# One Mamba scan with a routed feed-forward layer: two more of the 32 state terms of a block on ScalarE, the two parts of y added by TensorE, and a shifted table of slots

## The reference

```python
xz = xn @ in_proj_w.T                    # x_s and z, 512 channels each
u  = silu(conv4(x_s) + conv_b)
dt, B, C = split(u @ x_proj_w.T)         # 16, 16, 16
delta = softplus(dt @ dt_proj_w.T + dt_proj_b)
h = exp(delta * A) * h + delta * u * B   # per channel and each of 16 states, over time
y = sum over the states of h * C  + u * D_param
attn = (y * silu(z)) @ out_proj_w.T + residual
ffn  = top-2 of 8 experts, each (silu(x @ w1) * (x @ w3)) @ w2
x = x + attn + ffn
```

## Time and profile before

| what | value |
|---|---|
| median of 3 runs | 2661.89 us (2659.11 to 2669.71) |
| the profiled execution, its own time | 2653.93 us |
| its span | 2652.2 us |
| VectorE busy | 2459.2 us, 93% |
| TensorE busy (matmul) | 2292.8 us, 86% |
| GpSimd busy | 2031.0 us, 77% |
| ScalarE busy | 1658.9 us, 63% |
| mean granted TensorE clock | 0.936 |

### The profile page before, as it was taken

One profiled execution on the slowest core, in us unless ns is written; L12 is line 12 of the kernel. 1 busy time (PEld: TensorE's weight loads), 2 busy tenths in 40 slices (PEclk: granted clock), 3 DMA queues, 4 the chain that ended last, 5 costly groups with the idle time before them and its releaser, 6 DMA issues. The chain is left out here.

```text
span 2652.2 us, 47132 instructions
## 1 busy us (share of the span) xinstructions
PE 2292.8 (86%) x14442; PEld 1986.7 (75%) x14442; DVE 2459.2 (93%) x4041; ACT 1658.9 (63%) x4137; POOL 2031.0 (77%) x1607
## 2 busy tenths in 40 slices
PE   3958789899999999998999989999989899998665
PEld 2855578878787887877888877888877787887554
DVE  7679999999999999999999999999999999999997
ACT  3940566666666666666666666666666666666653
POOL 3430678888888888888888888888888888888883
PEclk7858899999999999999999999999999999999776
DMA  7216045565555555555555555555555555542451
GB/s 244 92 40 216 29 124 156 154 176 152 161 151 152 157 160 171 158 157 153 155 160 155 166 163 151 158 156 160 154 162 164 156 152 157 159 113 52 96 100 32
DMA packets 267099, 379.38 MB, mean 143 GB/s; under 512 B 21492, under 2 KB 158324, under 8 KB 266852
## 3 DMA queue, kind: packets, MB, share of 16 engines
q1 hardware_dynamic: 236196, 332.26, 40.2%
q0 software_dynamic: 28480, 43.94, 10.1%
q10 hardware_dynamic: 2176, 0.18, 0.1%
HBM read 332.59 MB, written 52.10 MB: 145 GB/s over the span
## 5 line engine op out<-in xcount | busy, mean ns | idle before, releaser
L475 POOL TENSOR_TENSOR h<-du,bbc 128x512 f32<-128x512 f32 x1024 | 1362.5, 1354 | 505.3 <-PE HT L1305 375.3
L1071 DVE TENSOR_TENSOR_SCAN h<-DA,carry,h 128x256 f32<-128x256 f32 x2048 | 1417.7, 734 | 91.4 <-ACT DA L748 79.0
L748 ACT ACTIVATE DA<-delta,alog 128x256 f32<-128x256 f32 x2048 | 882.6, 468 | 212.2 <-DVE h L1071 200.9
L1305 PE MATMUL HT<-ident,h 128*128 128x128 f32 x4096 | 665.8, 288 | 260.5 <-DVE yT L1082 259.1
L1305 PEld LDWEIGHTS HT<-ident,h 128*128 128x128 f32 x4096 | 496.6, 148 | 416.2 <-issue 375.2
L1082 DVE SCALAR_TENSOR_TENSOR yT<-HT,cT,yT 128x512 f32<-128x512 f32 x960 | 698.5, 728 | 3.1 <-PE HT L1305 3.1
L1354 PE MATMUL G<-xtT,W 128*128 128x128 f32 x2160 | 273.2, 281 | 0.0
L1368 PE MATMUL G<-W,fill 128*128 128x256 f32 x1080 | 271.8, 397 | 0.0
L1361 PE MATMUL G<-xtT,W 128*128 128x128 f32 x2160 | 263.4, 275 | 0.0
L1354 PEld LDWEIGHTS G<-xtT,W 128*128 128x128 f32 x2160 | 261.1, 198 | 0.0
L1361 PEld LDWEIGHTS G<-xtT,W 128*128 128x128 f32 x2160 | 252.2, 192 | 0.0
(11 more groups left out here) (183 smaller groups left out, 2986.6 us busy)
## 6 DMA issues: line engine op xcount, KB each, us to landing
W<-in_w_T_dram SPq DMA_DIRECT2D x405, 512.0 KB, 4.2
bbc<-b_dram SPq DMA_DIRECT2D x256, 256.0 KB, 4.3
xraw<-in_x_dram SPq DMA_DIRECT2D x64, 256.0 KB, 2.7
xn_dram<-W SPq DMA_DIRECT2D x8, 1032.0 KB, 14.0
W<-in_x_dram SPq DMA_DIRECT2D x32, 256.0 KB, 6.7
moe_dram<-fill SPq DMA_DIRECT2D x32, 256.0 KB, 4.0
out_dram<-tmpA SPq DMA_DIRECT2D x32, 256.0 KB, 2.2
out_dram<-moe_dram POOLq DMA_DIRECT2D x32, 256.0 KB, 4.4
```

Source lines behind the costliest of these rows:

```text
L475: pool.tensor_tensor(h[:, v % RING], du[:, b, 2 * q:2 * q + 2, :], bbc[:, s // 2 % BRING, s % 2, :].unsqueeze(1).to_broadcast([P, 2, T]), ...
L748: i = act.activation(DA[:, v % 2, k, :], delta[:, b, c, :], ACT.Exp, scale=nega[:, c, s:s + 1])
L1071: i = dve.tensor_tensor_scan(h[:, v % RING, k, :], DA[:, v % 2, k, :], h[:, v % RING, k, :], carry[:, b, s, c:c + 1], ALU.mult, ALU.add)
L1305: i = pe.transpose(HT[:, k, c * P:(c + 1) * P], h[:, (2 * s + c // 2) % RING, c % 2, k * P:(k + 1) * P], ident[:, :])
```

## The change

The terms u = 24 and 25 (state 12) are also made by ScalarE, in every block but the first. `first_state` becomes `state(j, b, u)`. The new terms go into their own buffer yS, which lies in a scratch area, with table entries second0 = 27 and second1 = 28. VectorE's adds of these two terms are gone; it has none in steps 28 and 29 any more. In `y_mm` each matmul of yT against the identity is preceded by one of yS, into the same sum: four more in each of the two calls. `by_act` and `added` say which terms are ScalarE's and which semaphore count stands for a term.

The table moves too: normalise 6 to 3, xs1 10 to 9, exp 22 to 21, ln 23 to 22, sp0 and sp1 24, 25 to 23, 24, wm 23 to 22, corr 24 to 23, delta 26 to 25, du 27 to 26, cT 25 to 24 and its copy 26 to 25, out1 29 to 28, result 31 to 30. `SCATTER` is 9 instead of 8. `MULT`, `Y` and `YO` are now given for each tile of a block: the first tile's are one step later (5, 6, 7), and so are the fourth tile's Y and YO (6, 7).

```diff
+        yS = scratch[4].rearrange("p (k d) -> p k d", k=NT)
...
-                 "first0": 3, "first1": 4, "y0": 4, "gate_y0": 6, "y1": 5, "gate_y1": 7, "out0": 27, "out1": 29,
-                 "oacc": 17, "result": 31,
-                 "normalise": 6, "transpose": 7, "copy_xT": 8, "xs0": 8, "copy_xs0": 9, "xs1": 10, "copy_xs1": 12,
+                 "first0": 3, "first1": 4, "second0": 27, "second1": 28, "y0": 4, "gate_y0": 6, "y1": 5, "gate_y1": 7, "out0": 27, "out1": 28,
+                 "oacc": 17, "result": 30,
+                 "normalise": 3, "transpose": 7, "copy_xT": 8, "xs0": 8, "copy_xs0": 9, "xs1": 9, "copy_xs1": 12,
                  "conv0": 11, "conv1": 12, "conv2": 13, "conv3": 14, "tanh_u0": 13, "silu_u0": 14, "tanh_u1": 15, "silu_u1": 16,
-                 "x_proj": 17, "copy_xdbc": 18, "dt": 19, "abs": 20, "exp": 22, "ln": 23, "sp0": 24, "sp1": 25,
-                 "wm": 23, "corr": 24, "delta": 26, "du": 27, "cT": 25, "copy_cT": 26}
+                 "x_proj": 17, "copy_xdbc": 18, "dt": 19, "abs": 20, "exp": 21, "ln": 22, "sp0": 23, "sp1": 24,
+                 "wm": 22, "corr": 23, "delta": 25, "du": 26, "cT": 24, "copy_cT": 25}
...
+        def by_act(n):
+            return (0, 1, 24, 25) if n else (0, 1)
+        def added(n, u):
+            if u < 0:
+                n, u = n - 1, u + U
+            if n < 0:
+                return s_acc, 0
+            mine = sum(i <= u for i in by_act(n))
+            earlier = 4 * n - 2 if n else 0
+            if u in by_act(n):
+                return s_y0, earlier + mine
+            return s_acc, U * n - earlier + u + 1 - mine
...
-        XT, XT_COPY, H1, H3, TANH, A2, MULT, Y, YO, SCATTER = 0, 1, 2, 3, 3, 4, 4, 5, 6, 8
+        XT, XT_COPY, H1, H3, TANH, A2, SCATTER = 0, 1, 2, 3, 3, 4, 9
+        MULT, Y, YO = (5, 4, 4, 4, 4), (6, 5, 5, 6, 5), (7, 6, 6, 7, 6)
...
-                act.activation(yT[:, b, k, :], HT[:, k, :], ACT.Identity, scale=cT[:, b, k, 0:1]).then_inc(s_y0, 1)
+                wait(act, s_ymm, 2 * (n - 1) if s == 0 else 2 * n)
+                if n == 1 and s:
+                    act.wait_ge(s_idx, 1)
+                act.activation(yS[:, k, :] if s else yT[:, b, k, :], HT[:, k, :], ACT.Identity,
+                               scale=cT[:, b, k, s:s + 1]).then_inc(s_y0, 1)
...
-                if u in (2, 3):
-                    pe.wait_ge(s_y0, 2 * n + u - 1)
-                else:
-                    wait(pe, s_acc, 30 * n + u - (1 if u < 2 else 3))
+                wait(pe, *added(n, u - 2))
...
+                        if n:
+                            pe.matmul(dst[:, m, k * P:(k + 1) * P], yS[:, k, c * P:(c + 1) * P], ident[:, :],
+                                      start=False, stop=False, skip_group_check=True)
                         i = pe.matmul(dst[:, m, k * P:(k + 1) * P], yT[:, b, k, c * P:(c + 1) * P], ident[:, :],
                                       start=False, stop=True, skip_group_check=True)
```

More of the change, by code:

```diff
@@ L240, in tile_of @@
             for k in range(PER):
-                at = U * (k // len(XT_UNITS)) + XT_UNITS[k % len(XT_UNITS)] + stage
+                at = U * (k // len(XT_UNITS)) + XT_UNITS[k % len(XT_UNITS)]
+                at += stage[k % len(XT_UNITS)] if isinstance(stage, tuple) else stage
                 for pair in (0, 1, -1):
@@ L698, in copy_cT, with state @@
                 act.wait_ge(s_btmm, n + 1)
-                wait(act, s_acc, 30 * (n - 1))
+                wait(act, *added(n - 2, U - 1))
                 act.copy(cT[:, b], FB[:, :, R + NS:ROWS]).then_inc(s_ct, 1)
-            def first_state(j, b, k):
+            def state(j, b, u):
                 n = number(j, b)
-                act.wait_ge(s_htr, 32 * n + k + 1)
+                s, k = divmod(u, 2)
+                act.wait_ge(s_htr, 32 * n + u + 1)
                 act.wait_ge(s_ct, n + 1)
-                wait(act, s_ymm, 2 * (n - 1))
-                act.activation(yT[:, b, k, :], HT[:, k, :], ACT.Identity, scale=cT[:, b, k, 0:1]).then_inc(s_y0, 1)
+                wait(act, s_ymm, 2 * (n - 1) if s == 0 else 2 * n)
[3 more added lines that the diff above has]
+                               scale=cT[:, b, k, s:s + 1]).then_inc(s_y0, 1)
             def abs_dt(j, b, q):
@@ L806, in step @@
                         if due(f"first{k}", v):
-                            first_state(j, b, k)
+                            state(j, b, k)
+                        if due(f"second{k}", v) and number(j, b):
+                            state(j, b, 24 + k)
                     tile_step(j, b, v)
@@ L1080, in add_state @@
                 if s == 1:
-                    dve.wait_ge(s_y0, 2 * n + k + 1)
+                    dve.wait_ge(*added(n, k))
                 i = dve.scalar_tensor_tensor(out=yT[:, b, k, :], in0=HT[:, k, :], scalar=cT[:, b, k, s:s + 1],
@@ L1153, in step @@
                     tile_a2(j, b, v)
-                    if (u := lagged(j, b, v, LAG)) and u[1] > 1:
+                    if (u := lagged(j, b, v, LAG)) and u[1] not in by_act(number(*u[0])):
                         add_state(*u)
@@ L1310, in y_mm @@
                 n = number(j, b)
-                pe.wait_ge(s_acc, 30 * (n + 1))
+                pe.wait_ge(*added(n, U - 1))
+                pe.wait_ge(*added(n, by_act(n)[-1]))
                 pe.wait_ge(s_z, 2 * n + q + 1)
```

## The result

The changed kernel takes 2745.81 us (median of 4 runs, 2743.25 to 2747.75) against 2664.3 us for the kernel before in the same comparison: a ratio of 1.0305, 95% interval 1.0281 to 1.0329. The direction was right, the size was not. I had forecast 2714 us and a range up to 2732. The profiled span is 2741.5 us, 89 us longer than before.

What follows compares the result with a forecast made beforehand. VectorE was taken to set the pace, with GpSimd second bound in steps 23 to 31. Terms of +0.9 (steps 0 to 21) and +1.2 us (22 to 31) over 27 blocks, less 5, gave 2714 us, range 2638 to 2732.

Steps and rivals of the forecast that it cites:

- The adds: VectorE, steps 28 and 29: two adds of 0.65 us go, -1.30 us a block, alone -40 us over 31 blocks.
- VectorE's own way through steps 22 to 31: VectorE's time there without GpSimd as the bound: 24.8 us, from 25.30 before.
- The decay of step 24: ScalarE, behind the earlier ln: VectorE waits 1.5 us there, where it waited 0.4 at step 25, +1.1 us.
- a drain: ScalarE's two table loads around ln: the sum left out some 1.38 us each, which would add some 30 us.
- the sum over steps 22 to 31: GpSimd's longer list before h(0) sets the stretch: 26.5 us, +1.2 us a block.
- the term for the blocks at the two ends: The four or so blocks without expert tiles lose only the adds: -5 us.
- The idle time beside the late decay: Steps 22 to 31: no cost was counted for TensorE idling while VectorE waits at step 24.
- rival (d): Waiting at step 31 idles TensorE some 3 us, its clock falls, z0 and H1 come late: 2738 us, chance 0.07.
- h(0) behind one scatter more: GpSimd, steps 22 to 31: the second tile's scatter joins the list before h(0), priced at 1.2 us with its issue.
- The added matmuls: TensorE, steps 4 and 5: +1.78 us a block, partly absorbed by spare time, leaving +0.9 us.
- The later MULT: First tile, step 8: it saves the 0.51 us wait for H3, eaten by a 1.3 us wait for the tanh.
- normalise in step 3: ScalarE: steps 5 and 6 come some 0.7 us late, counted 0 because VectorE waits for TensorE in step 8 anyway.

Runs made afterwards that it cites:

- e9: The kernel before, its table kept, with state 12's two terms on ScalarE instead of VectorE and no yS matmuls: 2652.24 us, ratio 0.9970.
- e2: The kernel before with only the ten softplus entries of the table (exp to du, cT and its copy) one step earlier: 2733.66 us, ratio 1.0277.
- e5: The changed kernel with the transposes of step 22 made six times and those of step 24 three times: 2739.04 us, ratio 1.0276.
- e7: The changed kernel with only wm, corr, delta and du back at steps 23, 24, 26 and 27: 2737.06 us, ratio 1.0285.
- e6: The changed kernel without the yS matmuls, so state 12's part of y is left out: 2702.45 us, ratio 1.0143.
- e4: The kernel before's table and tile stages, with state 12's two terms on ScalarE and the added matmuls: 2703.89 us, ratio 1.0153.
- e8: The kernel before with only the first tile's MULT, Y and YO one step later and xs1 in step 9: 2638.80 us, ratio 0.9907.
- e12: The kernel before with the first tile's MULT, Y, YO later, xs1 in step 9 and normalise in step 3: 2658.93 us, ratio 0.9994.

## Why the prediction was right in kind and too small

**Right, with its number.** The adds are worth 0.65 us each and 62 of them go, but VectorE's own way through steps 22 to 31 is not what sets their end: e9 shows 8 us for 40 us of work. VectorE does not wait for ScalarE behind the two new terms. Exp is only 0.9 us earlier in time. The decay of step 24 is 1.50 us late, 1.5 forecast. The sum was right to leave out a drain: in the changed kernel too the ln starts 0.01 us after the load (1110.12 + 1.28 and 1111.41, the same as in the earlier trace rows). The Trainium skill ("ScalarE: Activation LUTs", What ACT_TABLE_LOAD costs) puts 1.38 us of drain on top of each load; this trace does not agree, and the measurement decides. GpSimd idles 3.37 us ahead of h26, 3 forecast, and h31 ends 24 us after step 22, 24.1 forecast. Steps 0 to 21 take 52.57 us in the cycle shown and 52.71 in the mean, 52.4 forecast; TensorE has no wait at step 9 any more, and the tanh is 0.86 us late at step 8, 1.3 forecast.

**The step that failed** is the sum over steps 22 to 31 and the term for the blocks at the two ends. I had the stretch become 26.5 us, +1.2 a block; it takes 27.2 us (+1.9 on the 25.30 of the earlier trace rows) where GpSimd holds it and 27.7 to 28.0 where the clock does. Against the mean of the kernel before, which had late H1s already, it is +1.8. Two terms were wrong:

- *The idle time beside the late decay,* a term that I put at nothing. I had VectorE wait 1.5 us at step 24 and followed only VectorE. TensorE's transposes in steps 24 and 25 wait for the adds behind that decay, 1.62 and 1.66 us, on top of the 2.25 us that it waits there anyway. The low clock then falls on H1 of the fourth tile, which is needed two steps later, in 20 of 26 cycles, 7 before. e2 shows this without the rest of the change, e5 shows it away when TensorE is kept busy. On top of GpSimd's list it costs 0.24 us a cycle in the mean in steps 22 to 31 (27.42 and e5's 27.18); alone it would cost as much as the list (e7). My rival (d) had a falling clock, but at step 31 and with a chance of 0.07. In the cycle from 1187.60, where steps 31 and 0 do wait for GpSimd, TensorE's pauses there are 1.25 and 0.74 us and its clock stays up.
- *h(0) behind one scatter more.* This is the larger part: 26.5 forecast, 27.2 measured. I priced a scatter at 1.2 us, from its start to the start of the product behind it. But that product's record begins while the scatter's still runs, and lasts 1.84 us in place of 1.28; the earlier trace rows already had this at 1021.72. So for GpSimd the rule of reading from start to start does not hold: the overlap behind a scatter is 0.5 us, not a tenth. What stands behind a scatter is done 0.6 us later than the starts suggest, and a scatter costs about its whole 1.63 us. In the new order a scatter also stands directly ahead of h(0): h(0) starts at 1212.84, and VectorE's scan can start at 1214.79, 27.2 us after step 22. The forecast's own sum gave 1028.7 - 1002.02 = 26.7, which it carried on as 26.6 and then 26.5; the rest, 0.5, is about what the scatter was priced too low.

In steps 0 to 21 the terms were right in sum and wrong in their parts. The added matmuls cost 1.5 to 1.8 us a block (e6, e4), not 0.9. The later MULT gives back 0.73 (e8), which I had counted as eaten, and normalise in step 3, which I had counted as 0, takes 0.29 (e12). That the sum came out at 52.57 for a forecast of 52.4 is luck.

**The end** was forecast 5 us shorter and is 11 us longer. Shown of it: the last two y_mm calls take 1.8 us more, and in each of the last three blocks the result, now in step 30, waits 0.98 us for out1, which it never did before. e12 has 3 us more at the end than e8, for normalise alone. e5, e7 and e6 range from 232 to 243 us there, and which entry carries the remaining few microseconds stays open. The mark itself moved by a step, from 31 to 30; counted by VectorE's scans, the part ahead of step 22 of the third block is 3.5 us longer and the part behind the 26 cycles 9.3. In the sum: 27 x 2.9 + 11 = 89 us on the span, where I had 27 x 2.1 - 5 = 52.

## What to carry to other kernels

When one engine's wait grows by a microsecond, follow it to TensorE as well: with three short pauses within ten microseconds the halved clock fell on a matmul group that was on the path, where before it had mostly fallen on one that nobody waited for. Read more than one cycle: the one I built the forecast on was among the 19 of 26 that this did not touch. Before taking work off the busiest engine, look at what arrives with no slack at the end of that stretch; two bounds within half a microsecond of each other hide one another, and removing either shows almost nothing. In a table of steps written by hand, try each moved entry alone: here one move gained 25 us in the median and three others lost 16 to 25 each.

## What was not expected of the hardware

Five microseconds of granted clock 0.50 after pauses of 2.25, 1.62 and 1.66 us; with repeated transposes that left pauses of 1.62 and 0.79 it stayed at 1.00 in all 26 cycles of e5. In neighbouring blocks of the changed kernel the clock was low at different steps, at 1119.4 in one and at 1193.6, two steps earlier in its cycle, in the next, and in 2 of 26 cycles it did not fall in steps 22 to 31 at all. So cycles of equal work took 79.7 to 80.9 us, and 76.8 to 78.1 in the kernel before. On GpSimd the record of a product right behind a scatter starts 0.5 us before the scatter's ends and lasts 1.84 us, 1.28 otherwise, so only its end can be used to price what comes next.
